# A two-layer graph network: layer 0's ring of 20 spans, the softmax's row stage as one scan over two partitions, and one more TensorE product per step in layer 1

## The chip, the core and the metric

The kernel runs on one core of one Trainium2 chip. The metric is the device time of one execution in microseconds (us). Engines: PE is TensorE (with PEld for its weight loads), DVE is VectorE, ACT is ScalarE, POOL is GpSimd, SP is SyncE, which here only starts DMAs. All data are 32-bit floats.

## What is computed

The input is a graph with 12500 nodes of 256 features and 200000 edges sorted by destination, with 8 heads of 32 features. The two layers differ in how an edge's score is made; in both, a softmax over the edges of each destination node weighs the source nodes' values.

```python
# layer 0, h = relu(layernorm(x))
score = einsum('ehd,ehd->eh', K[src], Q[dst]) / sqrt(HD) + edge_bias
m = segment_max(score, dst); ex = exp(score - m[dst])
out = segment_sum(ex / denom[dst] * V[src], dst)
h1 = layer_norm(h + out @ Wp + bp); x = x + layer_norm(h1 + gelu(h1 @ W1 + b1) @ W2 + b2)
# layer 1, h = relu(layernorm(x)) @ W_lin + b_lin
feat = h @ W_gat; el = sum(feat * attn_l); er = sum(feat * attn_r)
e = leaky_relu(el[src] + er[dst], 0.2)
a = exp(e - segment_max(e, dst)[dst]) / denom[dst]
x = x + h + leaky_relu(segment_sum(feat[src] * a, dst) + gat_bias, 0.01)
```

## The kernel before

**Stages.** A setup with a pass over the 98 node tiles makes the tables of keys, values and queries. Then comes layer 0's edge phase, a second pass over the node tiles (the feed-forward part and layer 1's table), layer 1's edge phase, and a final pass.

**Steps and blocks.** Edges are cut into 782 spans of 256 (two chunks of 128, one edge to a partition). A step handles one span against one tile of 128 destination nodes; there are 880 steps, since a span that crosses into the next tile is handled twice. Eight steps (ST = 8) make a block, 110 blocks in each layer (NB). The code is unrolled: each engine's program goes through `turn(B)` of `edge_phase`, with s = 0 to 7, in a fixed order written by hand; engines meet at semaphores only.

**POOL** (`gathers`) issues two indirect DMAs for each span, which fetch the source rows of its two chunks into a slot of a ring in SBUF. The ring `Gf` has `SLOTS = (18, 32)` slots of spans in layers 0 and 1. Before it uses a slot again POOL waits for `ev_made` of the last step that read it, and it is at most 2 spans (layer 0) or 4 spans (layer 1) ahead of the landings that it announces (`LAND`). SP passes them on as `rows_rdy`.

**A step on the others.** PE: `spread` copies the destination nodes' rows to the edges (a product of a one-hot matrix with `qs`, 256 columns, in layer 0; with `erq`, 8 columns, in layer 1), for the step that comes two later; `agg` sums the weighted rows per node (264 columns for each chunk) for the step 12 earlier. In layer 0 `turns` transposes four one-hot matrices every second step. A 32-bit product that isn't a transpose is two MATMUL instructions with two weight loads. DVE in layer 0: `product` and `reduce` make the scores, `weigh` makes `ev` (rows times exponentials) for the step 12 earlier and `add` adds PE's sums for the step 14 earlier. In layer 1 `el_er` and `members` (a comparison that makes one-hot matrices) stand in place of `product` and `reduce`. ACT makes the one-hot matrices `oh` and, in layer 0, copies the transposed ones.

**A block's softmax.** After the eighth step the block's scores S (128 partitions by 8 heads times 16 chunks) are transposed by PE, so that a row has a head's chunk. DVE scans each row forwards and backwards (`chunk_scans`, s = 0). The rows' ends then go into one partition: PE transposes three columns (`row_values`, s = 0), ACT copies 1 x 384 values (`row_values`), DVE scans them forwards into U and backwards into Y and subtracts them into `ct` (`row_scans`, s = 1); ACT copies U and Y into `xy`, PE turns them back to columns (`columns`, s = 1), DVE scans all rows with these starts (`whole_scans`, s = 2), PE transposes the result (`maxima_turned`, s = 2), DVE subtracts (`below_maximum`, s = 3) and ACT takes the exponential (`weights`, s = 3) for the first `weigh` at s = 4. Aside, ACT makes `rexp` from `ct` (s = 2), PE spreads it over the partitions (`rescale`, s = 3), and ACT makes `rm` of it (`factors`, s = 4), which DVE needs at s = 6.

## Time and profile before

| what | value |
|---|---|
| median of 3 runs | 5988.14 us (5988.13 to 6003.22) |
| profiled execution | 5990.54 us, its span 5988.6 us |
| busy share of the span | PE 91%, DVE 82%, POOL 63%, ACT 53% |
| layer 0's edge phase | about 367 to 2690 us |
| layer 1's edge phase | about 3659 to 5768 us |

The span runs from the first to the last instruction of the profiled execution. Busy time is the time in which an engine has an instruction running; a PE that is busy is not a PE at its peak, since matmuls are pipelined and their ends are modelled. The granted clock (PEclk) is a share of 2.4 GHz, so 1.00 is 2.4 GHz and 0.50 is 1.2 GHz. The time behind an instruction in brackets is how long its engine had been idle, and what ended it; "issue" is nothing that the profile shows.

### The profile page before, as it was taken

To read this page: it belongs to the slowest core of one execution; us is meant where nothing else is said; L and a number is where in the kernel's file an instruction comes from. 1 tells how busy PE (TensorE), PEld (TensorE's weight loads), DVE (VectorE), ACT (ScalarE), POOL (GpSimd) and SP (SyncE) were. 2 spreads that over 40 slices of the span, in tenths; PEclk is the share of its full clock that TensorE was granted. 3 is DMA by queue.
4 is the path that set the end of the run, shared out by engine and by line. 5 is a ranking of instruction groups with operands and counts; after the bars stand their busy time and mean duration, and the time that the engine had idled before them with its cause. 6 is when DMAs were issued, how large, how long until landed. Compare 5 with 4: busy or idle time off the path is not lost.

```text
span 5988.6 us, 127287 instructions
## 1 busy us (share of the span) xinstructions
PE 5460.7 (91%) x26094; PEld 4327.4 (72%) x26094; DVE 4924.3 (82%) x12464; ACT 3152.8 (53%) x10275; POOL 3747.5 (63%) x4022
## 2 busy tenths in 40 slices
PE   8978888888888888888999998999999999999988
PEld 5556666666666666667999996777777777777766
DVE  4469999999999999996777775887888788878864
ACT  3446666666566566643333334555555555655533
POOL 1147776666667666644444446777777777777733
PEclk9999999999999999999999997777777777767789
DMA  5668898888888888872222224777777777777767
GB/s 177 212 222 290 286 290 284 286 287 282 287 283 288 286 284 283 288 234 83 85 85 85 84 83 140 221 218 222 218 220 218 219 218 218 220 218 219 218 201 230
DMA packets 723026, 1313.61 MB, mean 219 GB/s; under 512 B 109088, under 2 KB 502132, under 8 KB 722421
## 3 DMA queue, kind: packets, MB, share of 16 engines
q0 software_dynamic: 200192, 634.41, 36.8%
q1 hardware_dynamic: 444802, 422.18, 23.4%
q10 hardware_dynamic: 77426, 250.73, 10.9%
q14 instruction: 444, 3.63, 0.2%
q8 instruction: 162, 2.65, 0.2%
HBM read 964.16 MB, written 342.73 MB: 218 GB/s over the span
## 4 chain that ended last, share of the span: by engine, by line
PE 37%; DVE 30%; issue 18%; POOL 5%; DMA 4%; DVEq 3%; SPq 2%; ACT 2%; POOLq 1%; ACTq 0%
PE bank L816 35%; DVE sred L1199 7%; DVE prod L1193 7%; DVE ev L1284 5%; DVE acc L1299 4%; POOL Gf L525 3%; DMA Gf<-ft_tab,srcs 3%; PE bank L819 2%; POOL Gf L576 1%; DVE U L1251 1%; DVE Y L1252 1%; DVE scan L1261 1%; DVEq L1181 1%; DVEq L1284 1%; DVE scan L1239 1%
## 5 line engine op out<-in xcount | busy, mean ns | idle before, releaser
L816 PE MATMUL bank<-ev,oh 128*128 128x264 f32 x7040 | 2310.6, 459 | 88.7 <-DVE ev L1284 88.0
L525 POOL DMA_INDIRECT Gf<-kv_tab,srcs x1564 | 1570.4, 1004 | 724.1 <-issue 480.1
L525 POOL DMA_INDIRECT Gf<-ft_tab,srcs x1564 | 1598.9, 1022 | 483.2 <-issue 401.8
L816 PEld LDWEIGHTS bank<-ev,oh 128*128 128x128 f32 x7040 | 1480.0, 223 | 346.0 <-DVE ev L1284 123.4
L816 PE MATMUL bank<-Gf 128*128 128x128 f32 (+3 forms) x6480 | 1263.8, 346 | 22.1 <-ACT Gf L805 15.6
L1284 DVE TENSOR_TENSOR ev<-Gf,ex 128x528 f32<-128x528 f32 x1760 | 1232.9, 701 | 2.1 <-ACT ex L688 1.4
L816 PE MATMUL bank<-qs,oht 128*128 128x256 f32 x3520 | 954.8, 394 | 226.9 <-DVE prod L1193 226.6
L816 PEld LDWEIGHTS bank<-Gf 128*128 128x128 f32 x6480 | 967.2, 192 | 221.0 <-issue 98.5
L621 ACT ACTIVATE absd<-lane,dlocs 128x128 f32<-128x128 f32 x3520 | 1112.9, 389 | 4.0 <-DVE bms L1166 3.5
L816 PEld LDWEIGHTS bank<-qs,oht 128*128 128x128 f32 x3520 | 599.5, 190 | 437.6 <-issue 371.8
L1299 DVE SCALAR_TENSOR_TENSOR acc<-acc,same,bank 128x264 f32<-128x264 f32 x1540 | 736.0, 478 | 34.2 <-PE bank L816 30.8
L502 POOL TENSOR_TENSOR vr<-vr,mhalf 128x1 f32<-128x1 f32 x392 | 248.4, 634 | 717.6 <-DVE vr L1375 419.3
L626 ACT ACTIVATE oh<-absd,ones 128x512 f32<-128x512 f32 x880 | 631.6, 718 | 10.9
L1193 DVE TENSOR_TENSOR prod<-Gf,bank 128x512 f32<-128x512 f32 x880 | 597.9, 679 | 18.7 <-SPq L387 18.4
L1199 DVE TENSOR_REDUCE sred<-prod 128x16 f32<-128x512 f32 x880 | 593.9, 675 | 0.3
L582 ACT ACTIVATE oht<-bank 128x512 f32<-128x512 f32 x440 | 261.2, 594 | 300.0 <-PE bank L819 292.4
L816 PEld LDWEIGHTS bank<-erq,prod 128*128 128x128 f32 x1760 | 365.6, 280 | 62.5 <-issue 26.5
L770 ACT ACTIVATE Gf<-bank,Gf 128x128 f32<-128x128 f32 x784 | 223.7, 369 | 289.4 <-PE bank L816 289.4
L816 PE MATMUL bank<-erq,prod 128*128 128x8 f32 x1760 | 353.7, 311 | 14.6 <-DVE sred L1215 14.2
L652 ACT ACTIVATE rm<-bank,oh 128x8 f32<-128x8 f32 x220 | 78.6, 357 | 528.1 <-PE bank L816 525.1
L816 PEld LDWEIGHTS bank<-erq,oht 128*128 128x128 f32 x1760 | 269.5, 213 | 56.4 <-issue 25.4
L663 ACT ACTIVATE ats<-bank 128x128 f32<-128x128 f32 x220 | 61.0, 277 | 472.1 <-PE bank L819 472.1
(160 smaller groups left out, 6183.6 us busy)
## 6 DMA issues: line engine op xcount, KB each, us to landing
sums<-acc ACTq DMA_DIRECT2D x440, 528.0 KB
qs<-q_tab SPq DMA_DIRECT2D x880, 128.0 KB
qs<-dst_tab SPq DMA_DIRECT2D x880, 128.0 KB
Gf<-sums SPq DMA_DIRECT2D x196, 132.0 KB, 2.1
kv_tab<-Gf SPq DMA_DIRECT2D x98, 260.0 KB, 2.1
Gf<-in_x SPq DMA_DIRECT2D x196, 128.0 KB, 2.1
Gf<-kv_tab,srcs POOLq DMA_INDIRECT x1564
Gf<-ft_tab,srcs POOLq DMA_INDIRECT x1564
```

The lines of the kernel that those rows point to most:

```text
L502: pool.tensor_tensor(vr[:, 2 * k + 1:2 * k + 2], vr[:, 2 * k:2 * k + 1], mhalf[:, :], ALU.pow).then_inc(done, 1)
L525: pool.indirect_dma_start(out=rows[layer][:, m % SLOTS[layer], k, :], out_offset=None, in_=tab, in_offset=bass.IndirectOffsetOnAxis(ap=src ...
L582: act.activation(o, i_, ACT.Copy).then_inc(s, 1)
L621: act.activation(absd[:, g % 2, k, :], lane[:, :], ACT.Abs, scale=-1.0, bias=dloc[:, B.n, 4 * g + k:4 * g + k + 1]).then_inc(E_["ohd"], 1)
L626: act.activation(oh[:, B.tri, 4 * g:4 * g + 4, :].rearrange("p c n -> p (c n)"), absd[:, g % 2, :, :].rearrange("p c n -> p (c n)"), ACT.R ...
L770: act.activation(gT[:, f * P:(f + 1) * P], bank[2 + f // 4][:, (f % 4) * P:(f % 4 + 1) * P], ACT.Gelu, bias=v_b1[:, f:f + 1]).then_inc(S_[ ...
L816: return nc.tensor.matmul(o, a, r, start=first, stop=end)
L819: return nc.tensor.transpose(o, i_, ident[:, :])
L1193: V.tensor_tensor(prod[:, s % 2, :, :], step_rows(0, at)[:, :, 0:D], bank[2 + s % 2][:, :].rearrange("p (k n) -> p k n", k=2), ALU.mult).t ...
L1199: V.tensor_reduce(hc(sred[:, :])[:, :, 2 * s:2 * s + 2].rearrange("p h c -> p c h"), prod[:, s % 2, :, :].rearrange("p k (h w) -> p k h w" ...
L1284: V.tensor_tensor(ev[:, s % 4, :, :].rearrange("p k (h w) -> p k h w", h=H), val.rearrange("p k (h w) -> p k h w", h=H), hc(ex[:, B.par, : ...
L1299: V.scalar_tensor_tensor(acc[:, B.par, s, :], prev, same[:, B.n * ST + s:B.n * ST + s + 1], sums_bank(B, s), ALU.mult, ALU.add).then_inc(E ...
```

## The change

Four things change, all in the edge phases but for two constants at the start.

1. **Row stage.** The forward and the backward scan of the block's row values are now one scan over two partitions: partition 0 has the values forwards, partition 1 the same backwards. PE puts them there with four products (`ident` for one direction, the new `anti`, a mirrored identity, for the other) in place of three transposes. One DVE scan makes `uy`. The subtraction moves from DVE to PE: two products with rows of -1 and +1 (`minus_first`, `plus_second`) give the difference on all partitions at once, at s = 1 in `columns`; ACT's `rescale` moves to s = 4, and PE's `rescale` is gone.
2. **Ring.** Layer 0's ring has 20 slots for 18. The room comes from `oh`, now a ring of 10 groups of four one-hot matrices (16 chunks in 3 blocks before), and `ev`, 3 buffers for 4. ACT's `onehots` waits for `agg` of the step that read the group last.
3. **Layer 1's unread product.** In each step of layer 1 PE multiplies `ident` with the first half of `w_l` (256 columns) into bank 0, which nothing reads.
4. **Constants.** POOL makes `anti`, ACT makes `minus_first` and `plus_second` once, DVE clears three small columns.

```diff
-SLOTS = (18, 32)
+SLOTS = (20, 32)
-        oh = sb("oh", [P, 3, CH, P])
+        oh = sb("oh", [P, OHG, 4, P])
-        ev = sb("ev", [P, 4, 2, HV])
+        ev = sb("ev", [P, EVS, 2, HV])
...
             def onehots(B, g):
                 act.wait_ge(E_["ohd"], 16 * B.c + 4 * g + 4)
+                wait(act, E_["agg"], B.c * ST + 2 * g + 2 - 2 * OHG)
...
             def row_values(B):
                 act.wait_ge(E_["rows_mm"], B.c + 1)
-                copy(wlf[0:1, :, 1:].rearrange("p q (h c) -> p q h c", c=RW)[:, :, :, 0:CH],
-                     bank[7][0:1, 0:3 * P].rearrange("p (q h c) -> p q h c", q=3, c=CH), E_["rows_cp"])
+                copy(wv[0:2, :, 1:].rearrange("p q (h c) -> p q h c", c=RW)[:, :, :, 0:CH],
+                     bank[7][0:2, 0:2 * P].rearrange("p (q h c) -> p q h c", q=2, c=CH), E_["rows_cp"])
...
-                        if s == 2 and A.live:
+                        if s == 4 and A.live:
                             rescale(A)
-                        if s == 4 and A.live:
                             factors(A)
...
+            def unread():
+                mm(bank[0][:, 0:D], ident[:, :], w_l[:, 0, :])
...
                 pe.wait_ge(E_["scan_a"], 2 * B.c + 2)
-                for q, v in enumerate((wa[:, 0:1], scan1[:, P - 1:P], scan2[:, 0:1])):
-                    m = tr(bank[7][0:1, q * P:(q + 1) * P], v)
+                for q, (ahead, back) in enumerate(((wa[:, 1:3], wa[:, 0:2]), (last_0, first_0))):
+                    mm(bank[7][0:2, q * P:(q + 1) * P], ahead, ident[:, :], True, False)
+                    m = mm(bank[7][0:2, q * P:(q + 1) * P], back, anti[:, :], False, True)
...
                 pe.wait_ge(E_["xy_cp"], 2 * B.c + 2)
-                nc.tensor.transpose(bank[7][:, 384:385], xy[0:1, 0, :], ident[0:1, 0:1])
-                nc.tensor.transpose(bank[7][:, 385:386], xy[0:1, 1, :], ident[0:1, 0:1]).then_inc(E_["cols_mm"], 1)
+                mm(bank[7][:, 392:392 + H], minus_first[0:2, :],
+                   uy[0:2, :].rearrange("p (h c) -> p h c", c=RW)[:, :, 0], True, False)
+                mm(bank[7][:, 392:392 + H], plus_second[0:2, :],
+                   uy[0:2, H * RW - 1::-RW], False, True).then_inc(E_["r_mm"], 1)
+                mm(bank[7][:, 384:385], xy[0:2, 0, :], ident[0:2, 0:1])
+                mm(bank[7][:, 385:386], xy[0:2, 1, :], ident[0:2, 1:2]).then_inc(E_["cols_mm"], 1)
...
-            def rescale(B):
-                pe.wait_ge(E_["r_exp"], B.c + 1)
-                mm(bank[7][:, 392:392 + H], ones[0:1, :], rexp[0:1, :]).then_inc(E_["r_mm"], 1)
...
+                        if layer == 1 and B.live:
+                            unread()
...
-                r.did(V.tensor_tensor_scan(U[0:1, 0:n], w_[:, 0:n], l_[:, 0:n], -BIG, ALU.add, ALU.max))
-                r.seq(V.tensor_tensor_scan(Y[0:1, n:0:-1], w_[:, n:0:-1], f_[:, n:0:-1], -BIG,
-                                           ALU.add, ALU.max))
-                r.did(V.tensor_tensor(ct[:, :], y_[:, :, 0], u_[:, :, 0], ALU.subtract))
-                r.end()
+                V.tensor_tensor_scan(uy[0:2, :], wv[0:2, 0, 0:H * RW], wv[0:2, 1, 0:H * RW], -BIG,
+                                     ALU.add, ALU.max).then_inc(E_["row"], 1)
```

The order below is DVE's in a block of layer 0, s = 1 and the start of s = 2, before the change (`U`, `Y` and `ct` are the row stage, `acc` is `add`, `ev` is `weigh`; "ISA" loads a register).

```order
L1199 TENSOR_REDUCE sred<-prod 128x2x8
L1251 SCALAR_TENSOR_TENSOR U<-wlf 1x136
L1252 SCALAR_TENSOR_TENSOR Y<-wlf 1x136
L1256 TENSOR_TENSOR ct<-Y,U 1x8
L1299 SCALAR_TENSOR_TENSOR acc<-acc,same,bank 128x264
L1193 ISA
L1193 TENSOR_TENSOR prod<-Gf,bank 128x512
L1284 ISA
L1284 TENSOR_TENSOR ev<-Gf,ex 128x528
```

And this is the same place in the changed kernel, with one more row.

```order
L1225 TENSOR_REDUCE sred<-prod 128x2x8
L1273 SCALAR_TENSOR_TENSOR uy<-wv 2x136
L1316 SCALAR_TENSOR_TENSOR acc<-acc,same,bank 128x264
L1219 ISA
L1219 TENSOR_TENSOR prod<-Gf,bank 128x512
L1301 ISA
L1301 TENSOR_TENSOR ev<-Gf,ex 128x528
L1278 SCALAR_TENSOR_TENSOR scan<-ats,bank 128x128
```

Two of three instructions of the row stage are gone; nothing else moved on DVE.

PE's order in the same block of layer 0 before, from `row_values` at s = 0 to the product of `rescale` at s = 3 (`wa` and `scan` with one row are the row values, `xy` the columns, `rexp` the product of `rescale`, `ev,oh` is `agg`, `qs,oht` is `spread`).

```order
L819 MATMUL bank<-ident,wa 1x128
L819 MATMUL bank<-ident,scan 1x128 x2
L816 MATMUL bank<-qs,oht 128x256 x2
L816 MATMUL bank<-ev,oh 128x264 x2
L919 MATMUL bank<-ident,xy 128x1
L920 MATMUL bank<-ident,xy 128x1
L819 MATMUL bank<-ident,oh 128x128 x4
L816 MATMUL bank<-qs,oht 128x256 x2
L816 MATMUL bank<-ev,oh 128x264 x2
L819 MATMUL bank<-ident,scan 128x128
L816 MATMUL bank<-qs,oht 128x256 x2
L816 MATMUL bank<-ev,oh 128x264 x2
```

The same place after. Each row counts products, and each product is two MATMULs and two weight loads unless it is a transpose (L836).

```order
L833 MATMUL bank<-ident,wa 2x128
L833 MATMUL bank<-anti,wa 2x128
L833 MATMUL bank<-ident,scan 2x128
L833 MATMUL bank<-anti,scan 2x128
L833 MATMUL bank<-qs,oht 128x256 x2
L833 MATMUL bank<-ev,oh 128x264 x2
L833 MATMUL bank<-uy,minus_first 128x8
L833 MATMUL bank<-uy,plus_second 128x8
L833 MATMUL bank<-ident,xy 128x1 x2
L836 MATMUL bank<-ident,oh 128x128 x4
```

Three transposes of one column became four products, and two small transposes became four small products, of which the last two are those that DVE's next scans need.

PE's order in layer 1 after the change, s = 1 and s = 2 of a block. The rows with `steps,ident` are the new product (`w_l` lies in the tile `steps`); before, each pair of `erq` and `ev,oh` rows stood together.

```order
L833 MATMUL bank<-erq,prod 128x8 x2
L833 MATMUL bank<-steps,ident 128x256
L833 MATMUL bank<-ev,oh 128x264 x2
L836 MATMUL bank<-ident,scan 128x128
L833 MATMUL bank<-erq,prod 128x8 x2
L833 MATMUL bank<-steps,ident 128x256
L833 MATMUL bank<-ev,oh 128x264 x2
```

The new product waits for nothing and stands between `spread` and `agg` of every step.

## Rows read from the trace of the kernel before

**Rows 1.** Windows: both edge phases, busy time and instructions by engine

```profile
core 0: us, PE busy (x) PEld busy (x) DVE busy (x) ACT busy (x) POOL busy (x), PEclk, DMA share, GB/s
367.00:2690.00 2323.00, 2040.02 (x9900) 1579.38 (x9900) 2290.20 (x4624) 1387.10 (x4070) 1570.43 (x1564) 1.00 0.88 282
3659.00:5768.00 2109.00, 1958.51 (x8141) 1555.80 (x8142) 1675.23 (x4733) 1226.12 (x4504) 1598.90 (x1564) 0.72 0.76 216
```

**Rows 2.** Waits in layer 0, 400 to 2600: us in total, times, longest

```profile
DVE prod L1193 <- SPq L387: 3.0, 2, 1.6
...
PE bank L816 <- DVE prod L1193: 214.7, 318, 1.6
```

**Rows 3.** Timeline of layer 0, DVE: start us, us, instruction

```profile
1504.25 0.42 DVE L1251 TENSOR_TENSOR_SCAN U<-wlf 1x136 f32<-1x136 f32 x1
1504.60 0.40 DVE L1252 TENSOR_TENSOR_SCAN Y<-wlf 1x136 f32<-1x136 f32 x1
1505.03 0.16 DVE L1256 TENSOR_TENSOR ct<-Y,U 1x8 f32<-1x8 f32 x1
1505.12 0.48 DVE L1299 SCALAR_TENSOR_TENSOR acc<-acc,same,bank 128x264 f32<-128x264 f32 x1
...
1506.74 0.48 DVE L1261 TENSOR_TENSOR_SCAN scan<-ats,bank 128x128 f32<-128x128 f32 x1
```

**Rows 4.** Timeline of layer 0, PE and ACT, the same block

```profile
1500.42 1.10 PE L816 MATMUL bank<-qs,oht 128*128 128x256 f32 x4
...
1501.36 1.05 PE L816 MATMUL bank<-ev,oh 128*128 128x264 f32 x4
...
1502.25 0.27 PE L819 MATMUL bank<-ident,wa 128*1 128x128 f32 x1
...
1502.36 0.38 PE L819 MATMUL bank<-ident,scan 128*1 128x128 f32 x2
...
1503.26 1.10 PE L816 MATMUL bank<-qs,oht 128*128 128x256 f32 x4 [0.51 <-DVE prod L1193]
...
1505.25 0.29 ACT L582 ACTIVATE xy<-Y 1x128 f32<-1x128 f32 x1
...
1505.59 0.22 PE L919 MATMUL bank<-ident,xy 1*128 1x1 f32 x1 [0.34 <-ACT xy L582]
...
1505.68 0.20 PE L920 MATMUL bank<-ident,xy 1*128 1x1 f32 x1
...
1505.80 0.66 PE L819 MATMUL bank<-ident,oh 128*128 128x128 f32 x4
```

**Rows 5.** Timeline of layer 1, PE's weight loads of one `spread`

```profile
4519.10 0.53 PEld L816 LDWEIGHTS bank<-erq,oht 128*128 128x128 f32 x4
```

**Rows 6.** Chain of work that ended last, layer 1, shares by line

```profile
by line: PE bank L816 54.2%; issue 8.7%; DMA Gf<-ft_tab,srcs 7.6%; POOL Gf L525 6.9%; DVE ev L1284 6.2%; PE bank L819 2.6%; ACT wlf L582 1.6%; DVE U L1251 1.6%; POOLq L517 1.6%; DVE acc L1299 1.3%; DVE Y L1252 1.3%; DVE oht L1227 1.1%; DVE 
```

**Rows 7.** Lines of layer 1, 3659 to 5736: POOL's gathers

```profile
L525 POOL DMA_INDIRECT Gf<-ft_tab,srcs x1564 | 1598.9, 1022 | 483.2 <-issue 401.8 <-DMA Gf<-ft_tab,srcs 48.4 <-DVE ev L1284 32.9
```

**Rows 8.** Tile ft_tab: shortest, median, longest in ns, first and last start

```profile
L525 POOL DMA_INDIRECT Gf<-ft_tab,srcs x1564: 942/947/1501, 3660.1 to 5734.3; - x196
```

**Rows 9.** Waits in layer 1, 3700 to 5700: POOL, then DVE

```profile
POOL Gf L525 <- DVE ev L1284: 31.7, 104, 0.3
...
DVE scan L1239 <- PE bank L819: 136.6, 102, 3.2
```

**Rows 10.** Windows of 3 us in one block of layer 1

```profile
4502.00:4505.00 3.00, 2.58 (x18) 1.88 (x15) 2.87 (x11) 2.24 (x9) 2.39 (x3) 1.00 0.77 155
4508.00:4511.00 3.00, 2.66 (x7) 1.68 (x8) 3.00 (x9) 0.31 (x1) 2.47 (x2) 0.50 0.90 174
```

**Rows 11.** Timeline of layer 1, POOL and DVE, the same block

```profile
4507.99 0.70 DVE L1284 TENSOR_TENSOR ev<-Gf,ex 128x528 f32<-128x528 f32 x1
...
4508.22 1.28 POOL L525 DMA_INDIRECT Gf<-ft_tab,srcs  x1 [0.30 <-issue]
...
4509.81 1.25 POOL L525 DMA_INDIRECT Gf<-ft_tab,srcs  x1 [0.30 <-issue]
```

More of the change, by code:

```diff
@@ L45 @@
 WIDTH = (KVW, FTW)
-DIV = (1 << 16) // 18 + 1
+OHG = 10
+EVS = 3
+DIV = (1 << 16) // 20 + 1
 BIG = 1.0e30
@@ L87, in __init__ @@
         self.n, self.layer, self.c = n, layer, n + layer * NB
-        self.par, self.tri, self.half = n % 2, n % 3, n // 2
+        self.par, self.half = n % 2, n // 2
         self.live = 0 <= n < NB
@@ L273, in build @@
         accf = acc[:, :, :, :].rearrange("p a s n -> p (a s n)")
-        cmp_ = [(ohf if c < 4 else accf)[:, (c % 4) * NS:(c % 4 + 1) * NS] for c in range(LC)]
-        dsts = ohf[:, 4 * NS:6 * NS].bitcast(I32).rearrange("p (u k) -> p u k", k=2)
-        mtv = ohf[:, 4 * NS:6 * NS].rearrange("p (u k) -> p u k", k=2)
+        cmp_ = [(ohf if c < 5 else accf)[:, (c % 5) * NS:(c % 5 + 1) * NS] for c in range(LC)]
+        dsts = accf[:, 2 * NS:4 * NS].bitcast(I32).rearrange("p (u k) -> p u k", k=2)
+        mtv = accf[:, 2 * NS:4 * NS].rearrange("p (u k) -> p u k", k=2)
         prevs = lks[:, :, :].bitcast(I32)
@@ L611, in step_records @@
                 copy(o[:, 512:NS, e % 2], bank[7][:, 0:NS - 512], S_["x_cp"])
+            act.activation(minus_first[0:2, :], ident[0:2, 0:1].to_broadcast([2, P]), ACT.Copy,
+                           scale=-1.0).then_inc(E_["signs"], 1)
+            copy(plus_second[0:2, :], ident[0:2, 1:2].to_broadcast([2, P]), E_["signs"])
             for c in range(LC):
@@ L648, in factors @@
             def factors(B):
-                act.wait_ge(E_["r_mm"], B.c + 1)
+                act.wait_ge(E_["r_exp"], B.c + 1)
                 act.wait_ge(E_["oh0_made"], 2 * B.c + 2)
-                act.activation(rm[:, B.par, :], bank[7][:, 392:392 + H], ACT.Identity, scale=oh0[:, B.par, 0:1],
+                act.activation(rm[:, B.par, :], rexp[:, :], ACT.Identity, scale=oh0[:, B.par, 0:1],
                                bias=oh0[:, B.par, 1:2]).then_inc(E_["rm_made"], 1)
             def carried(B):
-                copy(wlf[0:1, 1, 0:H * RW].rearrange("p (h c) -> p h c", c=RW)[:, :, 0],
-                     U[0:1, 0:H * RW].rearrange("p (h c) -> p h c", c=RW)[:, :, CH], E_["carried"])
+                copy(wv[0:1, 1, 0:H * RW].rearrange("p (h c) -> p h c", c=RW)[:, :, 0],
+                     uy[0:1, :].rearrange("p (h c) -> p h c", c=RW)[:, :, CH], E_["carried"])
             def links(B):
@@ L873, in turns @@
                 for k in range(4):
-                    m = tr(bank[0][:, k * P:(k + 1) * P], oh[:, B.tri, 4 * g + k, :])
+                    m = tr(bank[0][:, k * P:(k + 1) * P], oh[:, (B.c * 4 + g) % OHG, k, :])
                 m.then_inc(E_["oht_tr"], 1)
@@ L955, in turn @@
                             maxima_turned(A)
-                        if s == 3 and A.live:
-                            rescale(A)
                         if s == 5 and B.live:
@@ L1065, in _ @@
             c0.did(V.memset(ats[:, P:P + 1], 0.0))
+            c0.did(V.memset(wa[:, :], 0.0))
+            c0.did(V.memset(scan1_0[:, P:P + 1], 0.0))
+            c0.did(V.memset(scan2_0[:, 0:1], 0.0))
             for kvo in kvos:
```

76 lines of the change are left out of this document (40 added, 36 removed).

## The prediction

> **What bounds the kernel now.** I read the windows by stage first, then who waits in each edge phase, then the timeline of one block of each, since the two phases have different limits. In layer 0's phase DVE is busy 2290 of 2323 us, PE 2040, POOL 1570, and PE's granted clock is 1.00, which is 2.4 GHz [rows 1]. DVE waits for rows 3.0 us in 2200, while PE waits 214.7 us for DVE's `prod` [rows 2]. The reader is to see one saturated engine and a PE that follows it: layer 0 is DVE's.
>
> Layer 1's phase looks otherwise: PE 1959 of 2109 us at a mean clock of 0.72, DVE 1675, POOL 1599 [rows 1]. The chain that ended last gives PE's `bank L816` 54% there [rows 6], and DVE waits 136.6 us in 102 blocks for a transpose of PE's [rows 9]. That points at PE. POOL's rows say another thing. Its 1564 gathers start from 3660.1 to 5734.3 us [rows 8], 2074 us in which it was busy 1598.9 and idle 483.2 [rows 7]. Of that idle time 6.9 us belong to the first gather; the rest is 0.305 us for each, and none of the 104 waits for `ev`, a slot that comes free, was longer than 0.3 [rows 9]. So POOL never waits for anything; 0.3 us between two gathers is what an issue costs. Median gather and gap give 1564 x (0.947 + 0.305) = 1958 us, and the mean of 1022 ns [rows 7] adds 1564 x 0.075 = 117: together the whole 2075. **Layer 1 is bound by POOL's issue of gathers**, and PE, however busy, trails it within a ring of 32 spans.
>
> A block of layer 1 takes 2075/110 = 18.9 us, and PE's clock alternates inside it: 1.00 at 4502 to 4505 and 0.50 at 4508 to 4511 [rows 10], so 2.4 and 1.2 GHz. Before it fell PE had gaps, 2.58 busy of 3.00 us.
>
> **The row stage on DVE, layer 0.** From the start of U to the start of `acc` it is 1505.12 - 1504.25 = 0.87 us. One scan keeps DVE 1504.60 - 1504.25 = 0.35 (the next instruction started then) [rows 3]. Two partitions for one cost at most little: the scan of `L1261` over 128 partitions and 128 elements takes 0.48, U's over one and 136 takes 0.42. Saved: 0.52 a block, 110 blocks: 57 us, if nothing takes it back.
>
> **What PE gets instead.** `row_values`: a 128-column transpose takes 1502.36 - 1502.25 = 0.11 [rows 4]. Four products of two such passes: 0.88 for 0.33, so +0.55. No duration of a two-column weight load with 128 columns behind it is at hand; the pass is the nearest row. This lies in cover: PE waited 0.51 for `prod` right behind it, at 1503.26 [rows 4], and PE's last row pass, over at 1502.36 + 0.38 = 1502.74 before and at 1503.3 now, leaves ACT 0.95 us for its copy before DVE's scan at 1504.25 (a copy of 128 values took 0.29).
>
> `columns`: eight pairs of a weight load and a tiny matmul for two. No row has a pair with two partitions. Bounds: the two transposes of `xy` start 0.09 apart (1505.59, 1505.68), four pairs of `spread` in layer 1 take 0.53, so 0.13 each [rows 4, 5], and a pair of 264 columns takes (1502.25 - 1501.36)/4 = 0.22 [rows 4]. I take 0.13, the same weights of 128 columns with 8 behind them: 1.04 us for 0.21. PE's `rescale`, two such pairs, goes: -0.26. In sum PE has 0.55 + 0.83 - 0.26 = 1.12 us more a block. It idles (2323 - 2040)/2323 of 20.8 us, 2.5 us; with 0.5 off the block 0.9 stays. PE does not become the bound.
>
> **What is late next.** DVE's `whole_scans` wait for the last of the eight pairs. Y ended at 1505.00 and the copies of `xy` at 1505.54; that is 0.54 behind the scan, so with the one scan ending at 1504.67 they end at 1505.21 and the first pair starts at 1505.26 (PE is free: spread from 1503.26 takes 1501.36 - 1500.42 = 0.94 and `agg` 0.89, to 1505.09) [rows 3, 4]. Eight pairs end at 1506.30, and a result is there some 0.15 later: 1506.45. DVE will want it at 1506.74 - 0.52 = 1506.22. It waits 0.23, and 0.29 of the 0.52 is left: **110 x 0.29 = 32 us for layer 0.** At 0.09 a pair (1506.13) nothing is lost, 57 us; at 0.22 the wait is 0.95 and layer 0 loses 110 x 0.43 = 47 us.
>
> **The ring of 20, `oh` and `ev`.** DVE waits 3.0 us for rows [rows 2]; two more slots can give no more than that. Without this cover (if DVE became faster than the gathers) the deeper ring would matter, but POOL's 1570 of 2323 us plus 1564 gaps of 0.305 is 2047, still 12% under the phase. `onehots`' new wait names `agg` of two steps back; behind it on ACT stand `turned` and `distances`. ACT already waits each second step of layer 0 for the transposes that PE issues after that `agg`: 0 us. In layer 1 ACT is busy 1226 of 2109 us [rows 1] and the matrices are used a dozen steps later: 0 us. `rescale` at s = 4 leaves DVE's need at s = 6: 0 us. Constants: two POOL instructions and some of DVE's ahead of the first DVE instruction, about +1 us.
>
> **Layer 1's product.** One product of 256 columns takes 0.94 / 2 = 0.47 us at 2.4 GHz [rows 4]. PE's work for a block is then 8 x (0.53 + 0.47 + 0.89) + 0.88 + 1.04 + 3 x 0.11 = 17.4 us of 18.9, 92% (before 12.5, 66%). It fits at 2.4 GHz and not at 1.2. I expect the clock to stay up, since layer 0 with 88% busy has it at 1.00 [rows 1] and what preceded the fall was a gap. Its direct worth is nothing, because PE isn't the bound.
>
> Indirectly it may be worth something. The 117 us of stretched gathers can move. A gather that started at 4508.22, 0.23 us after an `ev` of DVE (4507.99), took 1.28 for 0.95, and the next 1.25 [rows 11]. That stretch of DVE is a chase: fully busy for 3.00 us [rows 10] after waiting for PE at half clock, with steps of about the length of two gathers less one stretch, so that start meets `ev` again and again. If PE keeps up, DVE follows each landing at a fixed distance and meets POOL less often. The floor is 0 of the 117 us left; nothing says that it can't grow either, and three more stretches of 0.3 in each second block would be +50. I choose a third off, **40 us**, nearer the old value than the floor, since layer 0's DVE never chases and yet 1570 / 1564 = 1.004 us a gather is 57 ns over the 947 [rows 1].
>
> The Trainium skill (GPSIMD Engine Reference, Specifications) says that GpSimd's SBUF interfaces are shared with VectorE, with contention from VectorE instructions that have two SBUF inputs; `ev` is one, and the trace agrees. The skill (TensorE: Matmul & The Clock Gate, part 1) says that activity releases the throttle. By that rule alone, with PE taken as layer 1's bound from the chain, the step would follow PE: that is the fourth case below.
>
> **Sum.** Against the profiled execution's 5990.5: -32 - 40 + 1 = -71, 5919; the median of the runs is 2.4 lower, so **5917 us**. About 0.3% (18 us) is what a measurement tells from no change.
>
> **The cases.**
> 1. The forecast, both layers gain: 50%. Its own range 5870 to 5945.
> 2. Layer 1 stays at POOL's 2075 us with its stretches, whether or not the clock rises: -31, 5957. For it: nothing removes a gather, and layer 0, where PE waits for DVE, has stretches too. 24%.
> 3. PE's row stage eats DVE's saving: pairs at 0.16 put the last at 1506.69 and leave 0.05 of 0.52: -5, 5983. For it: no row has this pair. Against it: 0.13 has the same 128-column load. 9%.
> 4. PE's half clock costs more than I read, and all stretches go with it: POOL at its floor, -117 and -57: 5814. Against it: POOL has no wait to lose beyond these. 8%.
> 5. **Slower.** The clock in layer 1 goes on falling, and 17.4 us of work at the old mean of 0.72 takes 24.1 a block, 5.2 over POOL's 18.9: +570, less layer 0's 32: 6526. It decides below a mean clock of 17.4/18.9 = 0.92. For it: at 0.50 PE was busy for 2.66 of 3.00 us and the clock did not rise at once [rows 10]. Against it: a PE that lags has no gaps, and gaps preceded the fall; up to some 10 spans of the ring take a lag before POOL feels it. With `columns` at 0.22 a pair it is slower too, +47. 9% for both.
>
> The range leaves out half of cases 4 and 5 and part of the tails: 5860 to 5985. Faster is 1, 2 and 4 but for their tails, 0.80; the same 0.11; slower 0.09.
>
> **What would show it.** Layer 0: U and Y replaced by one scan of 0.42; U's start to `acc` 0.35; a wait of DVE for `xy`'s product of some 0.2 us, 110 times; PE pairs of 0.13; the block 20.5 for 20.8 us. Layer 1: the clock at 1.00 throughout, PE's busy share the same or higher, POOL's gathers still with gaps of 0.3 and no more, their mean under 1000 ns (floor 947), 2035 us from first to last start. I am wrong if POOL's gaps grow (it wasn't the bound, or PE now is), if the mean stays at 1022 with the clock up (the chase wasn't the cause), or if layer 0's block isn't shorter.

## The result

The changed kernel takes 6008.43 us in the median of 9 runs (6003.66 to 6022.65); the kernel before took 5994.03 beside it (5988.13 to 6003.22, 9 runs). The ratio is 1.0027, 95% interval 1.0018 to 1.0035: slower by about 14 us, where 5917 us was forecast, some 71 us less than the 5988 known then, in a range of 5860 to 5985. The profiled execution took 6006.19 us, its span is 6004.4.

The windows of the two edge phases of the changed kernel, same edges and columns as in [rows 1]:

```profile
367.00:2690.00 2323.00, 2151.30 (x10890) 1676.29 (x10890) 2244.22 (x4405) 1363.15 (x4070) 1570.24 (x1564) 1.00 0.88 282
3659.00:5768.00 2109.00, 1970.63 (x10869) 1585.96 (x10870) 1598.72 (x4502) 1211.20 (x4507) 1611.02 (x1564) 0.97 0.77 215
```

VectorE did lose its 46 us of work in layer 0 (2290.20 to 2244.22) and the clock did rise in layer 1 (0.72 to 0.97). Neither shortened its phase. The row stage in the timeline of layer 0, first VectorE, then PE (start us, us, instruction), answering to [rows 3, 4]:

```profile
1509.21 0.42 DVE L1273 TENSOR_TENSOR_SCAN uy<-wv 2x136 f32<-2x136 f32 x1
1509.56 0.45 DVE L1316 SCALAR_TENSOR_TENSOR acc<-acc,same,bank 128x264 f32<-128x264 f32 x1
...
1510.54 0.69 DVE L1301 TENSOR_TENSOR ev<-Gf,ex 128x528 f32<-128x528 f32 x1
1511.31 0.48 DVE L1278 TENSOR_TENSOR_SCAN scan<-ats,bank 128x128 f32<-128x128 f32 x1
```

```profile
1510.22 0.38 PE L833 MATMUL bank<-uy,minus_first 2*128 2x8 f32 x2
1510.47 0.36 PE L833 MATMUL bank<-uy,plus_second 2*128 2x8 f32 x2
1510.69 0.58 PE L833 MATMUL bank<-ident,xy 2*128 2x1 f32 x4
1511.20 0.65 PE L836 MATMUL bank<-ident,oh 128*128 128x128 f32 x4
```

Scan to `acc` is 1509.56 - 1509.21 = 0.35 us, as forecast, and the eight pairs take 1511.20 - 1510.22 = 0.98, 0.12 each. What is new stands in the waits of layer 0, 400 to 2600 (us in total, times, longest), against 3.0 us in 2 waits before [rows 2], and with POOL's and SyncE's:

```profile
DVE prod L1219 <- SPq L398: 39.5, 41, 2.1
```

```profile
SPq L398 <- POOLq L546: 823.2, 511, 7.0
SPq L386 <- PE bank L833: 14.8, 23, 1.3
```

```profile
POOL Gf L539 <- issue: 460.6, 1183, 4.4
POOL Gf L539 <- DVE ev L1301: 155.2, 170, 3.8
POOL Gf L539 <- DMA Gf<-kv_tab,srcs: 75.7, 150, 2.9
```

The reader is to see where the 46 us went: VectorE now waits for rows, SyncE hands rows on and itself waits for POOL's announcement of them, and POOL's idle time is issue, landings and 155.2 us under the name of `ev`, which the next reading shows to be no wait for VectorE. From the first `prod` of the layer to the last, VectorE is busy 2224.6 us for 2269.4 before and idle 61.3 for 17.1. The saving turned into a wait for gathers. In layer 1 the gathers still follow each other, as in [rows 7, 8]; the tile view of `ft_tab` (shortest, median, longest in ns, first and last start):

```profile
L539 POOL DMA_INDIRECT Gf<-ft_tab,srcs x1564: 942/947/1717, 3661.5 to 5748.0; - x196
```

That is 2086.5 us from first to last start, 12.4 more than before.

**A second reading of both traces.** Which span a step needs follows from the destination list (880 steps, 782 spans), so each of the 880 `prod` instructions can be set beside the gathers of its span, and each gather beside the `ev` that freed its slot. Per kernel, from the profiled execution: *stretch*, first gather's start to last one's end; *busy* of the 1564 gathers (some expectations below have it 2 us higher); *reload*, idle time over 0.3 us ahead of each eighth span, where POOL's queue reloads eight registers (`gathers`, `old % ST == 0`); *rows ahead*, mean time from the end of the last gather that must be issued before a span may be announced to the `prod` that needs it; *slot ahead*, mean time from a slot's last `ev` to the gather into it; *steps*, first to last start of `prod`; then layer 1's stretch, busy time, and gathers over 1.15 us. A single gather is called stretched when it takes clearly longer than the median of 0.946 us. Taken over every span, the two columns *ahead* come out up to 0.4 us different (8.0 and 3.6 before, 2.0 and 15.7 after).

| kernel | stretch L0 | busy | reload | rows ahead | slot ahead | steps | stretch L1 | busy | >1.15 us |
|---|---|---|---|---|---|---|---|---|---|
| before | 2280.3 | 1570 | 156 | 8.2 | 3.4 | 2286.5 | 2075.2 | 1599 | 279 |
| changed | 2286.3 | 1570 | 167 | 2.0 | 15.6 | 2285.9 | 2087.4 | 1611 | 312 |
| ring18 | 2284.7 | 1563 | 176 | 2.1 | 9.7 | 2284.3 | 2090.6 | 1614 | 326 |
| no_unread | 2281.3 | 1561 | 173 | 2.0 | 15.7 | 2280.9 | 2125.5 | 1649 | 403 |
| land3 | 2227.5 | 1525 | 155 | 12.5 | 1.8 | 2240.6 | 2088.9 | 1613 | 316 |
| land4 | 2227.7 | 1525 | 152 | 9.7 | 1.6 | 2240.7 | 2088.6 | 1612 | 310 |
| reload_early_c | 2235.7 | 1563 | 69 | 10.2 | 6.9 | 2242.8 | 2087.8 | 1611 | 308 |
| before_land4_c | 2277.3 | 1527 | 165 | 4.4 | 1.4 | 2284.6 | 2085.7 | 1609 | 304 |
| ex_bank0 | 2229.2 | 1526 | 152 | 9.7 | 1.6 | 2242.0 | 2002.3 | 1526 | 51 |

Before, rows lay ready 8.2 us ahead and a slot came free only 3.4 us ahead of its gather: POOL followed VectorE. After, rows lie ready 2.0 us ahead and slots 15.6: VectorE follows POOL. But POOL's stretch was 2280 us already. Before the change the two engines were within 1% of each other. No gather starts sooner than 0.81 us after the `ev` that freed its slot in any of these kernels, and in the changed kernel none sooner than 11.5: there the label `ev` names no real wait. Before, 41 gathers with idle time ahead of them started 0.81 to 1.3 us after it; these may have waited for a slot, 37 us in all.

### The profile page after: what moved, and what is told of

Same layout as the page of the kernel before. It is cut to its first block and busy times, and to the rows that moved or that the text cites. A ratio compares the mean times of both kernels' runs of the same rounds, so it can differ in the third digit from the quotient of the medians.

```text
span 6004.4 us, 135423 instructions
## 1 busy us (share of the span) xinstructions
PE 5594.9 (93%) x29834; PEld 4456.2 (74%) x29834; DVE 4836.0 (81%) x12027; ACT 3113.1 (52%) x10277; POOL 3759.6 (63%) x4024
## 5 line engine op out<-in xcount | busy, mean ns | idle before, releaser
L539 POOL DMA_INDIRECT Gf<-ft_tab,srcs x1564 | 1611.0, 1030 | 483.2 <-issue 421.7
L833 PE MATMUL bank<-ev,oh 128*128 128x264 f32 x7040 | 1893.7, 392 | 17.1 <-DVE ev L1301 5.7
L833 PEld LDWEIGHTS bank<-ev,oh 128*128 128x128 f32 x7040 | 1330.4, 192 | 288.2 <-DVE ev L1301 76.7
L833 PE MATMUL bank<-Gf 128*128 128x128 f32 (+3 forms) x6480 | 1265.3, 346 | 23.1 <-ACT Gf L822 15.6
L833 PE MATMUL bank<-steps,ident 128*128 128x256 f32 x1760 | 614.8, 432 | 0.0
L833 PEld LDWEIGHTS bank<-erq,oht 128*128 128x128 f32 x1760 | 243.8, 195 | 169.1 <-issue 140.2
L1241 DVE TENSOR_TENSOR sred<-Gf,bank 128x16 f32<-128x16 f32 x880 | 144.2, 164 | 278.2 <-SPq L398 274.0
L596 ACT ACTIVATE wv<-bank 2x256 f32<-2x256 f32 x220 | 82.4, 375 | 518.2 <-PE bank L833 516.2
L833 PE MATMUL bank<-erq,oht 128*128 128x8 f32 x1760 | 246.9, 249 | 96.0 <-DVE sred L1241 84.2
```

Source lines behind the costliest of these rows:

```text
L539: pool.indirect_dma_start(out=rows[layer][:, m % SLOTS[layer], k, :], out_offset=None, in_=tab, in_offset=bass.IndirectOffsetOnAxis(ap=src ...
L596: act.activation(o, i_, ACT.Copy).then_inc(s, 1)
L833: return nc.tensor.matmul(o, a, r, start=first, stop=end)
L1241: V.tensor_tensor(hc(sred[:, :])[:, :, 2 * s:2 * s + 2], step_rows(1, at)[:, :, HV:FTW].rearrange("p c h -> p h c"), bank[2 + s % 2][:, 0: ...
```

## Experiments

Each kernel is the changed one with one edit, if nothing else is said, in 5 to 12 timed executions; each ratio is against the kernel before on the same chip. The runs fell on seven chips. On four of them the kernel before took 5998 to 6001 us; on the other three it took 7390, 7390 and 7339, and the kernels timed there stand apart, at the end of this section.

**Landing depth in layer 0: land3, land4.** POOL waits for a span's landing, and announces it, after issuing two spans more. Edit: `LAND = (3, 4)` and `LAND = (4, 4)` for `(2, 4)`.

> The changed kernel with one more pair of gathers issued in layer 0 before their landing is waited for (3 in place of 2). Theory A (the gathers' own chain on POOL is the bound: 1572 us of gathers, 477 us of 0.3 us gaps, 167 us at the reload of eight registers before every eighth span, about 70 us of waits for landings): POOL's queue gets one span (2.5 us) further ahead, the reload of about 2.4 us is hidden but for a part, the gathers' stretch falls from 2286 us to 2130 to 2200, VectorE's 20.43 us a block (110 blocks, 2247 us, and about 30 us at the two ends) takes over, and the whole is 5965 to 5985 us. Theory B (the DMA engines, 0.89 busy, are the bound): the stretch stays within 5 us of 2286 and the time at 6008. Theory C (the rows' announcement one span later costs more than the reload): slower than 6008.

> The same with 4 in place of 2, as in layer 1, whose gathers show no gap at the reload. Theory A: the gap before every eighth span goes from 1.8 us to 0.3 us, as in layer 1, the gathers could end in about 2100 us and follow VectorE instead; layer 0's edge phase is set by VectorE's 20.43 us a block, 5960 to 5980 us in all. Theory B (DMA): 6008, with the reload's gap turned into waits for landings. Theory C (later announcement): slower than 6008, with VectorE's waits for rows growing by more than 40 us.

Measured: 5959.85 us, 0.9941 [0.9928, 0.9953], and 5958.46 us, 0.9935 [0.9922, 0.9947]. Theory A came nearest, the times 5 and 2 us below its ranges; B and C are out: the DMA engines were not the bound, since the gathers' stretch fell by 59 us with the same bytes (to 2228, and not into the 2130 to 2200 of land3's theory A). One detail failed. The idle time at the reloads did not go (155 and 152 us of 167). It costs nothing there, because POOL waits for slots again (1.6 us ahead; at 63 of land4's 89 longer reload gaps the gather starts within 1.0 us of the `ev` that freed its slot) and VectorE has the last word, 2241 us of steps. The reload therefore needed a test of its own.

**The reload alone: reload_early_c.** Depth 2 kept; the reload is written behind the gathers of span m, ahead of the wait for a landing.

```
+                    old = m + 1 - SLOTS[layer]
+                    if old >= 0 and old % ST == 0 and m + 1 < NSPAN:
+                        free = nc.values_load_multi_w_load_instructions(
+                            free_row[0:1, old:min(old + ST, NSPAN)], engines=[mybir.EngineType.Pool],
+                            min_val=layer * NS + 1, max_val=layer * NS + NS)[1]
                     n = m - LAND[layer]
                     if n >= 0:
                         pool.wait_ge(gat[n // ST % 2][n % ST], gathered(layer, n))
```

> The same kernel as in reload_early, likewise. Theory A, narrow form (the reload behind the landing's wait is what the gathers' chain can be rid of): 5955 to 5975 us and under 60 us at the reloads. Theory E (the landing's wait itself holds the queue, the reload only shows where it falls): 6000 to 6010 us, POOL waiting for a landing where it reloaded.

Measured: 5963.25 us, 0.9946 [0.9932, 0.9959]. Of 167 us at the reloads 69 are left, where under 60 were expected. Some 55 of the 98 came back as waits elsewhere in POOL's queue, which cost nothing, since VectorE has the last word again (2242.9 us of steps). Theory A holds in its narrow form: moving the reload alone takes 51 us off the stretch, 43 of idle time and 8 of busy. The reload ahead of span 356 in the timeline of POOL (start us, us, instruction, idle before), first the changed kernel, then the same four gathers of reload_early_c:

```profile
1408.83 0.95 POOL L539 DMA_INDIRECT Gf<-kv_tab,srcs  x1 [0.30 <-DMA Gf<-kv_tab,srcs]
1412.27 0.94 POOL L539 DMA_INDIRECT Gf<-kv_tab,srcs  x1 [2.49 <-issue]
1413.52 0.95 POOL L539 DMA_INDIRECT Gf<-kv_tab,srcs  x1 [0.30 <-issue]
1414.77 1.70 POOL L539 DMA_INDIRECT Gf<-kv_tab,srcs  x1 [0.30 <-issue]
```

```profile
1379.69 0.94 POOL L535 DMA_INDIRECT Gf<-kv_tab,srcs  x1 [0.30 <-issue]
1381.44 0.94 POOL L535 DMA_INDIRECT Gf<-kv_tab,srcs  x1 [0.81 <-issue]
1382.69 0.94 POOL L535 DMA_INDIRECT Gf<-kv_tab,srcs  x1 [0.30 <-issue]
1383.93 1.69 POOL L535 DMA_INDIRECT Gf<-kv_tab,srcs  x1 [0.30 <-issue]
```

The idle time falls from 2.49 to 0.81 us. The 2.49 us have no semaphore behind them ("issue"): the queue reads registers from 1408.65 to 1411.43, and the engine has nothing to do from 1409.78. The source view of that line in the changed kernel (count, shortest, median, longest in ns, both layers) prices it:

```profile
L531 POOLq FUSED_REGOPS  x1520: 147/147/182, 421.7 to 5728.8; - x190
L531 POOLq SEQ_ASSERT  x1520: 18/18/28, 421.9 to 5729.0; - x190
L531 POOLq TENSOR_LOAD <-slot_row x190: 567/577/2055, 420.9 to 5726.2; - x190
```

One load and eight of each of the others make 0.58 + 8 x (0.147 + 0.018) = 1.9 us. Elsewhere such a gap bears the name of `ev` (46 of 89 reloads in the changed kernel), though the slot had been free for more than 11 us.

**Who had the last word before: before_land4_c.** The kernel before with `LAND = (4, 4)`.

> The same kernel as in before_land4, for a chip on which the kernel before takes about 5995 us. Theory F (VectorE had the last word before the change, its rows lay ready 8.2 us ahead): 5985 to 5999 us; the row stage is then worth what lies between this kernel and land4, about 35 us. Rival G (the gathers were the bound before too, and the row stage saves nothing): 5950 to 5965 us.

Measured: 5995.09 us, 0.9992 [0.9983, 1.0001]. Theory F. Freeing the gathers alone gives nothing, the row stage alone gives nothing, both together give 0.9935. Between this kernel and land4, which differ by the change alone, the steps take 2284.6 and 2240.7 us (in the medians 37 us lie between them): **the row stage is worth 44 us, 0.40 a block**, once rows are there. The ring has no part in it, since VectorE waits for rows in neither, first before_land4_c, then land4, 400 to 2600:

```profile
DVE prod L1193 <- SPq L387: 1.8, 2, 1.6
```

```profile
DVE prod L1219 <- SPq L398: 1.1, 1, 1.1
```

**The ring: ring18.** `SLOTS = (18, 32)` and `DIV` for 18 again.

> The changed kernel with layer 0's ring at 18 spans again. Theory A: a slot of the ring of 20 is free 15.6 us (median) before its gather issues, so a ring two spans shorter still leaves about 10 us; no gather waits for a slot, and the time stays at 6008 within 4 us. A rival, that the two further spans are what moved the time (in either direction): 6008 plus or minus 15 us, with a gap of POOL's that ends with ev.

Measured: 6016.04 us, 1.0035 [1.0023, 1.0047], beside the changed kernel's 1.0027 [1.0018, 1.0035]. The time is 8 us over the expected 6008, where theory A allowed 4, but the intervals overlap and the steps take 2284.3 us for 2285.9. A slot was free 9.7 us ahead, never less than 5.8, and no gather waited for one: the two slots more did nothing in either direction that these runs can tell.

**The unread product: no_unread.** The call of `unread` taken out.

> The changed kernel without the product that nothing reads in layer 1. Theory A (layer 1 goes by POOL's issue of gathers; its 12 us more are gathers stretched by where the weighing instructions fall, which the faster PE moved): the clock falls back to about 0.7, the stretch of layer 1's gathers goes back from 2087 us to about 2075 and the time to 5993 to 5999. Rival D (the 12 us come from the new row stage or from the three ev buffers in place of four): the clock falls the same way and the time stays at 6008.

Measured: 6036.11 us, 1.0067 [1.0050, 1.0085]. Both theories missed: the product gives back 28 us in the medians, 24 by the ratios. Without it layer 1's clock is 0.80 and its gathers take 2125.5 us in place of 2087.4, all of it in busy time (1649 for 1611): 403 of them over 1.15 us for 312. POOL's gaps did not grow, so PE was no bound here either, and the worth is an indirect one, through the stretches. Against the kernel before (2075.2, and 2085.7 in before_land4_c, whose layer 1 is the same code) the row stage, the three `ev` buffers or what else changed beside the product had cost layer 1 some 40 to 50 us of stretched gathers, and the product took 38 of them back. Which of them it was, was not separated.

**What stretches gathers: ex_psum_land4_b, ex_bank0.** Both have landing depth 4. In ex_psum_land4_b layer 1's weights `ex` lie in PSUM banks 0 and 1, the sums share banks 4 and 5, and the product goes ahead of `agg`'s two into the same bank:

```
-            act.activation(ex[:, B.par, :], df[:, :], ACT.Exp)
+            act.activation(exs[B.layer][B.par], df[:, :], ACT.Exp)   # exs[1] = bank[0], bank[1]
+                if B.layer:
+                    wait(pe, E_["accd"], B.c * ST + s - 1)
+                    unread(s)
```

> The same kernel as in ex_psum_land4; in the eight runs before this one the kernel before took 7390 us, with idle times on every engine in the two unrolled stages. Beside a kernel before of about 5995 us: theory S, 0.972 of before (5830 us), layer 1's gathers at 955 ns with gaps of 0.3 us only; rival K, 0.98 to 0.995 of before, short gathers but longer gaps in layer 1, since PE's products now wait for the sums two steps back.

Measured: 6458.49 us, 1.0759 [1.0744, 1.0774]. The mechanism was right: 10 of layer 1's 1564 gathers take over 1.15 us, and the mean of all is 956 ns. The time was lost to rival K. The line of the gathers, and PE's longest group in the waits of 3900 to 5900:

```profile
L543 POOL DMA_INDIRECT Gf<-ft_tab,srcs x1564 | 1495.9, 956 | 1027.1 <-DVE ev L1306 606.1 <-issue 417.7 <-DMA Gf<-ft_tab,srcs 3.4
```

```profile
PE bank L837 <- DVE acc L1321: 315.4, 340, 1.1
```

PE waits for the add of two steps back, 0.93 us at a time. ex_bank0 therefore keeps three banks of sums. `ex` lies in bank 0 alone, the exponential waits for the last `ev` of the block before, and the product goes into the unused half of the bank of `spread`, ahead of its two products:

```
+                if B.layer:
+                    act.wait_ge(E_["ev_made"], B.c * ST)
+                act.activation(exs[B.layer][:, B.par, :], df[:, :], ACT.Exp)   # exs[1] = bank[0]
...
+                if layer == 1:
+                    unread(s)          # into bank[2 + s % 2][:, D:2 * D]
```

> The changed kernel with landing depth 4 in layer 0, and in layer 1 the weights ex in one PSUM bank that no product writes; the sums keep their three banks. The exponential waits for the last weighing of the block before, since both touch the bank, and the unread product goes into the other half of the bank that the next step's spreading products write, ahead of them. Theory S with the gathers as the bound: their mean is 955 ns and they follow each other with 0.3 us, layer 1's stretch falls from 2087 us to 1960 to 1990, the whole from land4's 5958 to 5835 to 5865 us, 0.975 of before. Rival K: PE, whose 282 of 300 us were busy, or VectorE's wait for the exponential is the next bound right behind, 5880 to 5950 us with waits of POOL for ev.

Measured: 5880.33 us, 0.9804 [0.9790, 0.9817], the fastest kernel of this study: 117 us under the kernel before, 78 under land4. Its gathers in layer 1, by line and by tile:

```profile
L541 POOL DMA_INDIRECT Gf<-ft_tab,srcs x1564 | 1525.9, 976 | 483.2 <-issue 421.4 <-DMA Gf<-ft_tab,srcs 40.8 <-DVE ev L1305 21.0
```

```profile
L541 POOL DMA_INDIRECT Gf<-ft_tab,srcs x1564: 942/946/1404, 3617.7 to 5619.1; - x196
```

The time lies above theory S's 5835 to 5865 and at the lower end of rival K's 5880 to 5950, but K's sign, POOL waiting for `ev`, is absent: the idle time is 483.2 us, the same number as in [rows 7], so neither PE nor VectorE came between. The mean fell from 1030 to 976 ns and not to 956, which is why the time missed. Of the 115 us by which the changed kernel's 1611.0 stood over ex_psum_land4_b's 1495.9, 85 are gone.

The kernel differs from land4 in three things (`ex`, the exponential's wait, the product's place), so the traces have to say which of them it was. In land4's layer 1, 276 gathers start within 0.4 us after an `ev` starts, and they take 90.0 us more than 0.947 each, of 131 us for all 1564. In ex_bank0 311 do, none takes over 1.15 us, and together they take no more than 0.947 each. Theory S holds: the weighing with two operands of SBUF is what stretches most gathers. Of the 51 that still take over 1.15 us, 50 start between 0.2 us before and 0.1 us after the start of `accr<-acc,rm`, once a block, another VectorE product of two SBUF operands. Moving that one was not tried.

**The chips with a slower kernel before.** The kernels below are those above, or new where marked, timed on three chips where the kernel before takes 7390.48, 7390.30 and 7338.71 us.

| run | us | ratio | gathers L1, mean ns |
|---|---|---|---|
| before_land4, before_land4_b | 7370.48, 7376.13 | 0.9971, 0.9967 | 1018, 1023 |
| before_unread, before_unread_b (new) | 7503.65, 7425.72 | 1.0149, 1.0120 | 1038, 1031 |
| reload_early, reload_early_b | 7823.98, 7834.19 | 1.0590, 1.0598 | 1043, 1043 |
| ex_psum, ex_psum_b, ex_psum_land4 | 8092.71, 8101.27, 8092.77 | 1.0957, 1.0947, 1.0936 | 955, 954, 953 |
| ex_bank0_no_unread (new) | 7589.08 | 1.0348 | 961 |

ex_psum has `ex` in two banks without the landing depth. before_unread is the kernel before with the unread product alone; ex_bank0_no_unread is ex_bank0 without it.

On the first of these chips:

> The changed kernel, landing depth 2 kept; the reload of eight registers on POOL's queue is written ahead of the wait for a landing, behind the last gather of the eight spans before, in both layers. Theory A in its narrow form (what binds layer 0's gathers is the reload, which POOL's queue can hide only if it isn't held up by the landing's wait first): the gap before every eighth span falls from 1.8 us to under 0.6 us, the 167 us at the reloads to under 60, and the whole lands where the landing depth of 3 did, 5955 to 5975 us. Theory E (the depth matters through the waits themselves and through how gathers fall against VectorE, the reload is no cost of its own): 6000 to 6010 us, and POOL waits for a landing where it reloaded before.

> The kernel before with a landing depth of 4 in layer 0, nothing else. Theory F (before the change VectorE, 20.82 us a block, and the gathers, 2280 us, bound layer 0 together to within 1 per cent; VectorE had the last word, its rows lay ready 8.2 us ahead): freeing the gathers alone gains nothing, 5990 to 5999 us. Rival G (the gathers alone were the bound before too, and the row stage saved nothing): 5950 to 5965 us, as with the change.

> The kernel before with the unread product of the changed one in layer 1, nothing else. Theory H (the product is worth its 28 us wherever it stands, since a PE at its higher clock keeps VectorE from running after lost time with its instructions close together, beside which gathers stretch): layer 1's gathers fall from 1601 us of busy time to about 1565, 5960 to 5975 us. Rival I (it only repairs what the new row stage or the three ev buffers brought into layer 1): 5990 to 6000 us.

> The changed kernel; in layer 1 the weights ex lie in two banks of PSUM in place of SBUF, so that the weighing reads one operand of SBUF and one of PSUM; the sums have two banks for three, and the unread product goes into the same banks, in order ahead of a step's two products. Theory S (gathers stretch where an instruction of VectorE with two operands of SBUF runs beside their start, and the weighing is nearly all of these): gathers over 1.15 us fall from 311 to under 60, their busy time from 1613 us to about 1500, layer 1's stretch from 2087 to 1970 or 1990 us, the whole to 5890 to 5910 us. Rival J (the stretch comes from VectorE's work as such, or from the transfers): the busy time stays over 1590 us and the time within 15 us of 6008. Rival K (another bound stands right behind POOL in layer 1, PE with its two banks): the gathers shorten but get gaps, 5960 to 6000 us.

On the second:

> The same kernel as in reload_early, timed again because the kernel before took 7390 us beside it there, with idle times of PE, VectorE and ScalarE that nothing in the profile explains. Beside a kernel before of about 5995 us: theory A, narrow form, 0.993 to 0.997 of before (5955 to 5975 us) with under 60 us left at the reloads; theory E, 1.002 to 1.003 of before and a wait for a landing where it reloaded.

> The same kernel as in before_land4. Theory F (VectorE had the last word before the change): within 0.3 per cent of before. Rival G (the gathers were the bound before too): 0.993 to 0.995 of before.

> The same kernel as in ex_psum. On the other chip layer 1's gathers took 955 ns (mean), against 1018 to 1043 in the three kernels beside it, layer 0's 963 in all four. Theory S: 1564 gathers of 955 ns and 470 us of gaps make layer 1's stretch 1964 us in place of 2087, the whole 5885 us, 0.981 of before. Rival K (PE with its two banks of sums, or VectorE, is the next bound in layer 1): gathers of under 970 ns, but gaps of more than 0.3 us between them, 0.99 to 1.00 of before.

> Both: the landing depth of 4 in layer 0 and ex in PSUM in layer 1. If the two stages are independent, the gains add: land4 gave 0.9935 of before against 1.0027 for the change alone, so this one is 0.009 below ex_psum's ratio, about 0.972 under theory S (5830 us) and 0.98 to 0.99 under rival K.

On the third:

> The same kernel as in before_unread, for a chip on which the kernel before takes about 5998 us. Theory H (the product is worth about 28 us wherever it stands): gathers of layer 1 at about 1575 us of busy time, 5965 to 5975 us. Rival I (it repairs only what the row stage brought into layer 1): 5990 to 6000 us, with gathers near 1600 to 1615 us.

> ex_bank0 without the unread product. Theory L (the product works through the gathers alone, by what it does to their stretches): with ex in PSUM there is little left to stretch, and the time stays at 5880 within 8 us though the clock falls to about 0.8 in layer 1. Rival M (PE at the lower clock is a bound of its own in layer 1): 5895 to 5925 us, with gaps of more than 0.3 us between gathers.

None of the times expected here can be read off these runs, since they were worked out for a kernel before of about 5995 us. The questions on the reload, on the kernel before with depth 4 and on `ex` in PSUM were settled by the later runs above.

One thing carries over: wherever `ex` lies in PSUM, layer 1's gathers take 953 to 961 ns, wherever it lies in SBUF 1018 to 1043, whatever the pace around them. The two questions on the product do not: both stages are paced there by something else (below), gathers have gaps of far more than 0.3 us in each of these kernels, and a gather's stretch costs nothing. Whether the product helps the kernel before (theory H), and whether it acts through the gathers alone (theory L), stays open.

## Why the prediction was wrong

**The step that failed** is in the part on the ring: "POOL's 1570 of 2323 us plus 1564 gaps of 0.305 is 2047, still 12% under the phase". It left out what stands between the gathers beside the issue. The gathers run from 369.2 to 2649.4 us, 2280 of 2323: 1570 busy, 477 of issue gaps, 156 at the 96 reloads, 78 in other waits. I made that count for layer 1, from the first and the last start, and not for layer 0, where VectorE's 2290 us looked like the whole answer. POOL's chain was 10 us shorter than VectorE's 2290 and 6 us shorter than its steps, so some 10 us were to be had at most, and not 32. None was: in the changed kernel, where no slot holds a gather back, the chain takes 2286 us, so what had been waits for slots came back at reloads and landings. No case of mine held it; the sentence names the danger ("if DVE became faster than the gathers") and dismisses it by the wrong sum. land4, reload_early_c and before_land4_c show it from three sides.

**The row stage** itself was right in its mechanism and undersized: 44 us for 32, once rows are there. The wait for `xy`'s product takes 0.16 us a block instead of 0.23: from the start of `ev` to that of the scan it is 0.775 us in the median of 109 blocks, for 0.619 before (in the rows above 1511.31 - 1510.54 = 0.77), with pairs of 0.12 for 0.13. The median block of layer 0 did fall as forecast, from 20.84 to 20.44 us; the mean, 20.83, did not, because VectorE waits for rows in the others. That was the prediction's own sign of being wrong. Case 3, the nearest to the measured time, had another mechanism, PE's pairs, which the 0.12 refutes.

**Layer 1** is bound by POOL's issue of gathers, as read: the clock went from 0.72 to 0.97 and the idle time stayed at 483.2 us. The term of -40 had the wrong sign. +12.2 us were measured in the profile, but before_land4_c, with layer 1 as before, had 2085.7 in its execution, so no more than 2 of them are surely the change's. The step that failed is "If PE keeps up, DVE follows each landing at a fixed distance and meets POOL less often". VectorE still runs after lost time, now behind the announcement: between 3700 and 5700 it waited for rows 38.5 us in the kernel before, most of its waits being for PE. The timeline of one block of the changed kernel:

```profile
4507.26 0.47 DVE L1316 SCALAR_TENSOR_TENSOR acc<-acc,same,bank 128x264 f32<-128x264 f32 x1
4510.15 0.17 DVE L1241 TENSOR_TENSOR sred<-Gf,bank 128x16 f32<-128x16 f32 x1 [2.43 <-SPq L398]
...
4512.28 0.69 DVE L1301 TENSOR_TENSOR ev<-Gf,ex 128x528 f32<-128x528 f32 x1
...
4513.83 0.69 DVE L1301 TENSOR_TENSOR ev<-Gf,ex 128x528 f32<-128x528 f32 x1
```

```profile
4512.55 1.24 POOL L539 DMA_INDIRECT Gf<-ft_tab,srcs  x1 [0.30 <-issue]
4514.09 1.24 POOL L539 DMA_INDIRECT Gf<-ft_tab,srcs  x1 [0.30 <-DMA Gf<-ft_tab,srcs]
```

Rows come 2.43 us late, then VectorE takes steps of 1.55 us, one gather of 1.24 and one gap of 0.30 fit each exactly, and the next gather again meets an `ev` 0.27 us old. In the changed kernel such waits add up to 252.6 us, 215 times:

```profile
DVE sred L1241 <- SPq L398: 252.6, 215, 3.7
```

The mean of a gather is 1030 ns with the mean clock at 0.97, which the prediction had named as a sign of being wrong, and 287 gathers start within 0.4 us after the start of an `ev`, as many as before (372 in no_unread): VectorE meets POOL no less often. In the block above it chases after a wait for rows and not for PE. ex_bank0, which takes the stretch away and not the meetings, is what gained. The clock did not stay at 1.00 either. Why the product is worth 28 us against no_unread stays open.

**Case 5** did not decide (0.97 is above 0.92), the constants cost 1.2 us for 1, and `oh`, `ev` and the ring show no wait in layer 0.

The rule of the Trainium skill (GPSIMD Engine Reference, Specifications), contention from VectorE instructions with two SBUF inputs, agrees with these runs: with one of `ev`'s inputs in PSUM the gathers' mean falls from 1030 to 976 ns.

## What to carry to other kernels

Before an edit takes time from the busiest engine, take the first and last start of every other engine's main group in that phase: an engine that is "68% busy" can have work from one end to the other, its gaps made of issue, register reloads and landings, and then it is the bound, 10 us behind. Where a queue waits for a landing in order, put register reads ahead of that wait, or let the landing lie one transfer deeper; either one turned this change from 0.3% slower into 0.5 to 0.7% faster, and the landing depth was worth nothing without the change. Where POOL's issue of gathers binds, look at which VectorE instruction beside it reads two operands of SBUF, and move one operand to a PSUM bank that PE does not write; taking a bank from PE's sums for it cost more than it gave (ex_psum_land4_b).

## What the hardware showed beyond this

**The stretch depends on the phase.** In layer 0 of the changed kernel, 81 gathers start within 0.2 us after the start of an `ev` and take 36.7 us more than 0.947 each; 52 start 0.2 to 0.4 after one and take 15.3 more; 115 at 0.4 to 0.6 only 5.1; from 0.6 to 1.2 us after one, 459 gathers take none. By tenths of a microsecond the mean excess is 0.51, 0.40, 0.32, 0.23, 0.11 and 0.03 us: the later a gather starts beside an `ev`, which takes 0.70, the less it loses. In land4, where slots come free shortly before their gathers, 22 start within 0.2 us and 61 at 0.2 to 0.4 (27.1 us more in all), and busy time fell by 46 us with no edit to either instruction.

**PE's clock.** In the block above, PE was busy 1.93 of 3.00 us at a granted clock of 1.00 while VectorE waited for rows; in the window after it, 3.00 of 3.00 at 0.50, so 2.4 and then 1.2 GHz (windows of the changed kernel, columns as in [rows 1]):

```profile
4506.00:4509.00 3.00, 1.93 (x11) 1.43 (x10) 1.69 (x4) 0.75 (x2) 2.38 (x3) 1.00 0.92 283
4511.00:4514.00 3.00, 3.00 (x9) 2.48 (x9) 3.00 (x9) 2.28 (x10) 2.19 (x2) 0.50 0.61 167
```

**Chips on which unrolled code is slower.** On three chips the kernel before took 23% longer. The windows of before_land4_b there, and of the kernel before here, in the looped first stage and in the unrolled layer 0:

```profile
100.00:300.00 200.00, 193.12 (x641) 107.06 (x642) 98.22 (x321) 82.94 (x258) 35.17 (x64) 1.00 0.64 211
...
700.00:1000.00 300.00, 232.06 (x1014) 177.36 (x1014) 236.71 (x475) 142.89 (x420) 154.59 (x160) 0.88 0.75 224
```

```profile
100.00:300.00 200.00, 193.16 (x641) 107.25 (x642) 98.20 (x321) 82.85 (x258) 35.03 (x64) 1.00 0.64 211
700.00:1000.00 300.00, 266.62 (x1300) 207.08 (x1298) 299.02 (x606) 181.55 (x534) 208.28 (x208) 1.00 0.90 288
```

The loop runs alike to the instruction, 641 in both; the unrolled stage issues 1014 PE instructions for 1300 (before_land4_c, the code of before_land4_b on a chip like the first four, issues 1300 as well), and every engine is less busy. What holds them up nothing here tested. The order of kernels is another one there: reload_early is 6% slower than the kernel before, ex_psum 9.5%.
